# Attention stage: turning before the scores, Y turned back one unit at a time, two buffers for Y^T

## Chip, cores, metric

One core of one Trainium2 chip. The metric is the device time of one execution in microseconds. The program is a chain of stages (four layers) in one launch; the change is in one stage, the attention of layer 0.

## What is computed

Layer 0 is a normalization, three projections, softmax attention with 4 batches of 1024 positions, 16 heads of 32, and an output projection. The stage at hand is this part:

```python
q = (xn @ q_w + q_b).reshape(Bx, Tx, H, -1)
k = (xn @ k_w + k_b).reshape(Bx, Tx, H, -1)
att = jnp.einsum('bnhl,bmhl->bnmh', q, k)
mask = src_mask.reshape(Bx, 1, Tx, 1)
att = att + (1.0 - mask) * -1000000.0
att = jax.nn.softmax(att, axis=2)
v = ((xn @ v_w + v_b) * src_mask[:, :, None]).reshape(Bx, Tx, H, -1)
y = jnp.einsum('bnmh,bmhl->bnhl', att, v).reshape(Bx, Tx, Dx)
```

The other stages (a linear attention, two selective scans, their projections) are not touched.

## The kernel before

The work of the stage is cut into units: one unit is 128 queries of one head of one batch, against all 1024 keys, so U = 4 x 16 x 8 = 512 units. Four units make a group (G = 128), two a pair. q, k and v come in two parts each, a high and a low one, so that products at TensorE's faster fp32r type are exact enough. The queue SP loads q and k (ring of three), v and the mask row.

There is no planner. Each engine's order is written out by hand as a loop over u, and semaphores (`w(engine, name, count)`) hold the engines together.

- **TensorE** (L749 to L816): `scores(u)` makes S in two matmuls of 512 columns, into one of two PSUM buffers, once `shifted` says that the unit two before has been read. `turn(u)` transposes the probabilities `pr` in eight transpositions of 128x128 into the single PSUM buffer TP; it waits for `exped` (the unit's exponential) and, half by half, for `lo_taken` (the half of TP is free). `weigh(u)` does eight matmuls of 256 columns, half of those of a pair, that sum v^T p^T into YT, high and low part in turn. `turn_back(g)` multiplies the copied Y^T of four units by `fold`, which adds the two 32-row halves and turns Y back, into the single PSUM buffer Y; it waits for `yt_copied` and `y_ready`. Its contraction runs over 64 rows, that of all the others over 128.
- **VectorE** (L818 to L862): `shift(u)` adds the mask, takes the maximum and writes `sm`; `take_lo(u)` makes the low part of p^T in two halves from TP and the high part; `take(g)` divides Y of four units by the sums of the exponentials (a reciprocal and a multiplication).
- **ScalarE** (L864 to L891): the exponential of a unit, `copy_hi(u)` (the high part of p^T in two halves, out of TP), and `copy_yt(g)` (YT to SBUF, `yts`).

In the loop of TensorE the scores are three units ahead, and the weighing two behind. In the loop of VectorE the low part is of the unit before, the shift two ahead. ScalarE does the exponential of u, then the high part of u - 1, and in every fourth unit the copy of Y^T.

Of the kernel before, what the change touches and what calls it, by code (L numbers as in the profile page):

```python
# [19 lines left out]
P = 128  # L20
B, T, D = 4, 1024, 512
E = 1024
H, DH = 16, 32
# [636 lines left out]
def attention(core, ident, io, scr):  # L660
# [3 lines left out]
    nc = core.nc  # L664
    with ExitStack() as ctx:
        sb, psum = allocator(nc, ctx, "att")
        ring = lambda n, count, shape: [sb(f"{n}{j}", shape) for j in range(count)]
# [3 lines left out]
        fold = sb("fold", [2 * DH, DH])  # L671
# [1 line left out]
        psums = sb("psums", [P, 16])  # L673
        pT = [ring(f"pT{part}", 2, [P, 2, T]) for part in ("hi", "lo")]
        rden = sb("rden", [P, 4])
        yts = sb("yts", [2 * DH, 4, P])
        y = ring("y", 2, [P, TT, D])
        S = [psum(f"S{j}", [P, T]) for j in range(2)]
        TP = psum("TP", [P, T])
        YT = psum("YT", [2 * DH, 4, P])  # L680
        Y = psum("Y", [P, 4, DH])
# [6 lines left out]
        U = B * H * TT  # L688
# [59 lines left out]
        @block.tensor  # L748
        def _(pe):  # L749
            def scores(u):  # L750
                n, t = u // TT, u % TT
                if t == 0:
                    pe.wait_ge(kq_in[n % 3].handle, kq_in[n % 3].at(128 * (n // 3 + 1)))
                if u >= 2:
                    w(pe, "shifted", u - 1)
                for c in range(2):
                    last = nc.tensor.matmul(S[u % 2][:, c * HALF:(c + 1) * HALF], q[n % 3][:, t * P:(t + 1) * P].bitcast(F32R),
                                            k[n % 3][:, c * HALF:(c + 1) * HALF].bitcast(F32R), start=True, stop=True)
                last.then_inc(s["scored"].handle, 1)

            def turn(u):
                w(pe, "exped", u + 1)
                for half in range(2):
                    if u >= 1:
                        w(pe, "lo_taken", 2 * u - 1 + half)
                    for m in range(4 * half, 4 * half + 4):
                        last = nc.tensor.transpose(TP[:, m * P:(m + 1) * P], pr[u % 2][:, m * P:(m + 1) * P], ident[:])  # L767
                    last.then_inc(s["turned"].handle, 1)

            def weigh(u):  # L770

                def of(pair, keys):
                    for m in keys:
                        for part in range(2):
                            last = nc.tensor.matmul(YT[:, pair * 2 % 4:pair * 2 % 4 + 2, :],  # L775
                                                    v[n // 4 % 2][:, m, n % 4, :].bitcast(F32R),
                                                    pT[part][pair % 2][:, :, m * P:(m + 1) * P].bitcast(F32R),
                                                    start=(m == 0 and part == 0), stop=(m == TT - 1 and part == 1))
                    return last

                pair, g = u // 2, u // 4
                n = pair * 2 // TT
                if u % 2 == 0:
                    w(pe, "lo_taken", 2 * u + 4)
                    if u % (4 * TT) == 0:
                        c = n // 4
                        pe.wait_ge(v_in[c % 2].handle, v_in[c % 2].at(16 * (c // 2 + 1)))
                    if u % 4 == 0 and g >= 1:
                        w(pe, "yt_copied", g)
                    of(pair, range(0, TT // 2))  # L790
                else:
                    of(pair, range(TT // 2, TT)).then_inc(s["weighed"].handle, 2)

            def turn_back(g):
                w(pe, "yt_copied", g + 1)
                if g >= 1:
                    w(pe, "y_ready", g)
                for n in range(4):
                    last = nc.tensor.matmul(Y[:, n, :], yts[:, n, :], fold[:], start=True, stop=True)
                last.then_inc(s["y_turned"].handle, 1)  # L800

            w(pe, "fold_ready", 1)
            scores(0)
            scores(1)
            scores(2)
            for u in range(U):
                if u + 3 < U:
                    scores(u + 3)
                turn(u)
                if u >= 2:  # L810
                    weigh(u - 2)
                if u >= 7 and u % 4 == 3:
                    turn_back((u - 7) // 4)
            weigh(U - 2)
            weigh(U - 1)
            turn_back(G - 1)  # L816

        @block.vector  # L818
        def _(dve):
            def shift(u):  # L820
                b = u // (H * TT)
                if u % (H * TT) == 0:
                    w(dve, "mneg_ready", b + 1)
                w(dve, "scored", u + 1)
                if u >= 2:
                    w(dve, "exped", u - 1)
                nc.vector.tensor_tensor_reduce(sm[u % 2][:], S[u % 2][:], mneg[b % 2][:], -1.0, HUGE,  # L827
                                               ALU.add, ALU.min, nmax[u % 2][:]).then_inc(s["shifted"].handle, 1)

            def take_lo(u):  # L830
                for half in range(2):
                    cols_ = slice(half * HALF, (half + 1) * HALF)
                    w(dve, "hi_copied", 2 * u + half + 1)
                    nc.vector.tensor_tensor(pT[1][u // 2 % 2][:, u % 2, cols_].bitcast(F32R), TP[:, cols_],  # L834
                                            pT[0][u // 2 % 2][:, u % 2, cols_], ALU.subtract).then_inc(s["lo_taken"].handle, 1)

            def take(g):
                b, h, first = g // (2 * H), g // 2 % H, g % 2 * 4
                at = g % 4 * 4
                w(dve, "y_turned", g + 1)  # L840
                nc.vector.reciprocal(rden[:], psums[:, at:at + 4]).then_inc(core.vector_step.handle, 1)
                dve.wait_ge(core.vector_step.handle, core.vector_step.at(g + 1))
                if g % (2 * H) == 0 and b >= 2:
                    dve.wait_ge(y_stored[b % 2].handle, y_stored[b % 2].at(16 * (b // 2)))
                nc.vector.tensor_tensor(y[b % 2][:, first:first + 4, h * DH:(h + 1) * DH], Y[:],
                                        rden[:].unsqueeze(2).broadcast_to([P, 4, DH]), ALU.mult
                                        ).then_inc(s["y_ready"].handle, 1)

            nc.vector.tensor_tensor(fold[:], ident[0:2 * DH, 0:DH], ident[0:2 * DH, DH:2 * DH], ALU.add
                                    ).then_inc(s["fold_ready"].handle, 1)  # L850
            shift(0)
            shift(1)
            for u in range(U):
                if u >= 1:
                    take_lo(u - 1)
                if u + 2 < U:
                    shift(u + 2)
                if u >= 9 and u % 4 == 1:
                    take((u - 9) // 4)
            take_lo(U - 1)  # L860
            take(G - 2)
            take(G - 1)  # L862

        @block.scalar  # L864
        def _(act):
            def copy_hi(u):
                if u >= 4:
                    w(act, "weighed", u // 2 * 2 - 2)
                for half in range(2):
                    cols_ = slice(half * HALF, (half + 1) * HALF)  # L870
                    w(act, "turned", 2 * u + half + 1)
                    nc.scalar.copy(pT[0][u // 2 % 2][:, u % 2, cols_].bitcast(F32R), TP[:, cols_]).then_inc(s["hi_copied"].handle, 1)  # L872

            def copy_yt(g):
                w(act, "weighed", 4 * g + 4)
                if g >= 1:
                    w(act, "y_turned", g)
                nc.scalar.copy(yts[:], YT[:]).then_inc(s["yt_copied"].handle, 1)

            for u in range(U):  # L880
                w(act, "shifted", u + 1)
                if u >= 2:
                    w(act, "turned", 2 * u - 2)
                if u % 4 == 0 and u >= 16:
                    w(act, "y_ready", u // 4 - 3)
                at = u % 16
                nc.scalar.activation(pr[u % 2][:], sm[u % 2][:], ACT.Exp, bias=nmax[u % 2][:, 0:1], scale=-1.0,  # L887
                                     accum_out=psums[:, at:at + 1]).then_inc(s["exped"].handle, 1)
                if u >= 1:
                    copy_hi(u - 1)  # L890
                if u >= 6 and u % 4 == 2:  # L891
                    copy_yt((u - 6) // 4)
            copy_hi(U - 1)
            copy_yt(G - 1)
# [1044 lines left out]
```

## Time and profile before

| | |
|---|---|
| median of 3 runs | 7576.78 us (7569.86 to 7577.42) |
| profiled execution | 7567.35 us |
| its span, first to last instruction | 7565.6 us |
| share of the span busy: PE, PEld, DVE, ACT, POOL | 80%, 54%, 66%, 59%, 33% |
| mean granted clock of TensorE over the span | 0.922 |
| attention stage, first turn to last | 576.6 to 1972.9 us |

PE is TensorE's matmuls, PEld its weight loads, DVE VectorE, ACT ScalarE. The costliest groups of the whole program are those of the scans, which lie in other stages; the rows below are of the attention stage, except where a row of another stage shows the same kind of step. Matmuls are pipelined and the end of one is modelled, so distances between starts are read, not durations. In the timeline neighbouring instructions of one kind are merged (x8), and a short stretch is asked for where single ones matter. "issue" is time in which the engine waited for nothing that the profile shows.

### The profile page before, as it was taken

The numbers are of one execution on the slowest core, as the hardware profiler recorded it, in microseconds if no ns is written. First come the engines' busy times: TensorE is split into PE (matmuls) and PEld (weight loads), VectorE is DVE, ScalarE is ACT, GpSimd is POOL, SyncE is SP. The second block draws the span as 40 slices with busy tenths as digits, with TensorE's granted clock in tenths as the row PEclk, the third lists the DMA queues.
The fourth block names the chain that finished last, engine by engine and source line by source line (L and its number), as shares of the span: only waits on it lengthen the run. The fifth ranks groups of instructions, "written<-read, shape, count | busy, mean of one in ns | idle before, by whom it ended". The sixth has DMA issues, their size and how long they took to land. (4 is left out here: it accounts for less than half of the span.)

```text
span 7565.6 us, 90723 instructions
## 1 busy us (share of the span) xinstructions
PE 6062.6 (80%) x31488; PEld 4117.5 (54%) x31488; DVE 5014.9 (66%) x6337; ACT 4501.4 (59%) x6759; POOL 2519.9 (33%) x1130
## 2 busy tenths in 40 slices
PE   4899999999568945599957888887499957888884
PEld 1338888888433443344436666665244446666662
DVE  2338999999541153344459999996344479999993
ACT  2118888888510042244458888885344469888991
POOL 0000000000000000000039999996100059999994
PEclk8999999999789977799979999999799979999997
DMA  5443232222353244533355555653433355655554
GB/s 192 192 155 77 64 75 73 65 68 62 122 191 138 94 165 182 200 124 147 121 164 139 154 147 160 161 153 92 163 128 132 135 165 145 163 154 149 149 150 164
DMA packets 615822, 1035.65 MB, mean 137 GB/s; under 512 B 105817, under 2 KB 253401, under 8 KB 608741
## 3 DMA queue, kind: packets, MB, share of 16 engines
q1 hardware_dynamic: 600484, 954.60, 41.3%
q10 hardware_dynamic: 9792, 58.85, 1.9%
q0 software_dynamic: 5120, 16.78, 0.6%
q8 instruction: 236, 3.87, 0.2%
q14 instruction: 190, 1.55, 0.1%
HBM read 640.74 MB, written 389.31 MB: 136 GB/s over the span
## 5 line engine op out<-in xcount | busy, mean ns | idle before, releaser
L1570 POOL TENSOR_TENSOR scan_hC<-scan_h,scan_Crep 128x1024 f32<-128x1024 f32 x1024 | 2395.0, 2367 | 3491.6 <-DVE scan_h L1740 3421.8
L1613 PE MATMUL scan_y<-ident,scan_hC 128*128 128x128 f32 x8192 | 1136.5, 283 | 369.6 <-POOL scan_hC L1570 365.1
L1690 ACT ACTIVATE scan_a<-scan_dt,scan_A 128x512 f32<-128x512 f32 x2048 | 1352.2, 694 | 48.9 <-DVE scan_h L1740 45.3
L1740 DVE TENSOR_TENSOR_SCAN scan_h<-scan_a,scan_carry,scan_h 128x512 f32<-128x512 f32 x1024 | 1220.0, 1261 | 57.7 <-ACT scan_a L1690 55.0
L1740 DVE TENSOR_TENSOR_SCAN scan_h<-scan_a,scan_h 128x512 f32<-128x512 f32 x1024 | 1161.1, 1201 | 109.7 <-ACT scan_a L1690 107.0
L1666 ACT COPY scan_h<-scan_drive 128x1024 f32<-128x1024 f32 x1024 | 1040.2, 1016 | 299.0 <-PE scan_drive L1601 279.9
L1613 PEld LDWEIGHTS scan_y<-ident,scan_hC 128*128 128x128 f32 x8192 | 908.3, 143 | 529.2 <-POOL scan_hC L1570 461.7
L1601 PE MATMUL scan_drive<-scan_Bd,scan_dT 128*128 128x256 f32 x4096 | 878.2, 337 | 138.3 <-ACT scan_h L1666 82.3
L1601 PEld LDWEIGHTS scan_drive<-scan_Bd,scan_dT 128*128 128x128 f32 x4096 | 598.8, 195 | 410.9 <-issue 248.6
L834 DVE TENSOR_TENSOR att_pTlo<-att_TP,att_pThi 128x512 fp32r<-128x512 f32 x1024 | 657.9, 684 | 128.3 <-ACT att_pThi L872 126.5
L872 ACT CAST att_pThi<-att_TP 128x512 fp32r<-128x512 f32 x1024 | 547.2, 586 | 179.7 <-PE att_TP L767 173.1
L827 DVE CUSTOM_DVE_ANT_0 att_sm<-att_S,att_mneg 128x1024 f32<-128x1024 f32 x512 | 621.5, 1214 | 13.0 <-POOL att_mneg L745 12.8
L887 ACT ACTIVATE att_pr<-att_sm,att_nmax 128x1024 f32<-128x1024 f32 x512 | 592.9, 1158 | 46.5 <-DVE att_nmax L827 46.5
L521 PE MATMUL p_bank<-p_W,p_xT 128*128 128x512 f32 x1280 | 557.7, 597 | 51.8 <-DMA p_xT<-scratch_xT 48.5
L767 PE MATMUL att_TP<-ident,att_pr 128*128 128x128 f32 x4096 | 566.6, 279 | 24.8 <-DVE att_pTlo L834 24.7
L767 PEld LDWEIGHTS att_TP<-ident,att_pr 128*128 128x128 f32 x4096 | 453.3, 141 | 184.9 <-issue 116.3
L1639 PE MATMUL scan_O<-scan_Wo,scan_gT 128*128 128x512 f32 x1024 | 536.9, 617 | 5.4 <-ACT scan_gT L1697 5.4
L775 PE MATMUL att_YT<-att_pThi,att_v 128*64 128x256 f32 x2048 | 538.6, 298 | 0.0
L1188 PE MATMUL ssmin_ring<-ssmin_xT,ssmin_Wx 128*128 128x512 f32 x1024 | 472.7, 619 | 70.4 <-DMA ssmin_xT<-scratch_xT 53.3
L775 PE MATMUL att_YT<-att_pTlo,att_v 128*64 128x256 f32 x2048 | 496.2, 277 | 0.0
L1188 PE MATMUL ssmin_ring<-ssmin_Wz,ssmin_xT 128*128 128x512 f32 x1024 | 459.2, 599 | 11.6 <-ACTq L1253 11.6
L745 POOL TENSOR_SCALAR att_mneg<-att_mrow 128x1024 f32<-128x1024 f32 x4 | 14.5, 3636 | 1348.8 <-DMA att_mrow<-mask 1348.8
(142 smaller groups left out, 6804.1 us busy)
## 6 DMA issues: line engine op xcount, KB each, us to landing
scan_dT<-scratch_dtuT SPq DMA_DIRECT2D x512, 256.0 KB, 4.9
scratch_dtuT<-ssmin_dT SPq DMA_DIRECT2D x128, 512.0 KB, 2.9
scan_Crep<-scratch_bc SPq DMA_DIRECT2D x64, 1024.0 KB, 10.7
scratch_xT<-n_xT ACTq DMA_DIRECT2D x24, 2048.0 KB, 7.4
p_xT<-scratch_xT SPq DMA_DIRECT2D x16, 2048.0 KB
att_q<-scratch_q_split SPq DMA_DIRECT2D x256, 128.0 KB, 3.0
att_k<-scratch_k_split SPq DMA_DIRECT2D x256, 128.0 KB, 3.2
scratch_uD<-ssmin_uD SPq DMA_DIRECT2D x64, 512.0 KB, 4.4
```

The source lines that it names most:

```text
L767: last = nc.tensor.transpose(TP[:, m * P:(m + 1) * P], pr[u % 2][:, m * P:(m + 1) * P], ident[:])
L775: last = nc.tensor.matmul(YT[:, pair * 2 % 4:pair * 2 % 4 + 2, :], v[n // 4 % 2][:, m, n % 4, :].bitcast(F32R), pT[part][pair % 2][:, :, m ...
L827: nc.vector.tensor_tensor_reduce(sm[u % 2][:], S[u % 2][:], mneg[b % 2][:], -1.0, HUGE, ALU.add, ALU.min, nmax[u % 2][:]).then_inc(s["shif ...
L834: nc.vector.tensor_tensor(pT[1][u // 2 % 2][:, u % 2, cols_].bitcast(F32R), TP[:, cols_], pT[0][u // 2 % 2][:, u % 2, cols_], ALU.subtract ...
L887: nc.scalar.activation(pr[u % 2][:], sm[u % 2][:], ACT.Exp, bias=nmax[u % 2][:, 0:1], scale=-1.0, accum_out=psums[:, at:at + 1]).then_inc( ...
L1188: last = nc.tensor.matmul(ring[o % 4][:], lhs, rhs, start=(kt == 0), stop=(kt == KT - 1))
L1570: nc.gpsimd.tensor_tensor(hC[k % 2][:], of, Crep[:, 2 * p:2 * p + 2, :], ALU.mult).then_inc(s["scaled"].handle, 1)
L1601: last = nc.tensor.matmul(drive[:, c * TC:(c + 1) * TC, :], dT[j][:, at * P:(at + 1) * P].bitcast(F32R), Bd[th][:, at, :, first:first + GS ...
L1613: last = nc.tensor.matmul(y[j][:, t, :], hC[k % 2][:, i, t * P:(t + 1) * P], ident[:], start=(p == 0 and i == 0 and t == 0), stop=False, i ...
L1666: nc.scalar.copy(h[group % 3][:, :, tt * P:(tt + 1) * P], drive[:].rearrange("p t n -> p n t")).then_inc(s["laid"].handle, 1)
L1690: nc.scalar.activation(a[(2 * k + i) % 3][:], dt[j][:], ACT.Exp, scale=A[:, m, 2 * p + i:2 * p + i + 1]).then_inc(s["decayed"].handle, 1)
L1740: nc.vector.tensor_tensor_scan(of, a[(2 * k + i) % 3][:], of, first, ALU.mult, ALU.add).then_inc(s["scanned"].handle, 1)
```

## The change

Three edits in `attention`. TensorE's loop calls `turn(u)` before `scores(u + 3)`, not after. `turn_back` works on one unit instead of four, in every round from u = 7 on, each raising `y_turned`; the waits stand before the first piece of a group. `yts` becomes a ring of two, and `copy_yt(g)` waits for the block of g - 2 instead of g - 1. VectorE's `take` moves from behind the shift in rounds with u % 4 = 1 to ahead of the shift in rounds with u % 4 = 3, and waits for four pieces.

```diff
-        yts = sb("yts", [2 * DH, 4, P])
+        yts = ring("yts", 2, [2 * DH, 4, P])
...
-            def turn_back(g):
-                w(pe, "yt_copied", g + 1)
-                if g >= 1:
-                    w(pe, "y_ready", g)
-                for n in range(4):
-                    last = nc.tensor.matmul(Y[:, n, :], yts[:, n, :], fold[:], start=True, stop=True)
-                last.then_inc(s["y_turned"].handle, 1)
+            def turn_back(u):
+                g = u // 4
+                if u % 4 == 0:
+                    w(pe, "yt_copied", g + 1)
+                    if g >= 1:
+                        w(pe, "y_ready", g)
+                nc.tensor.matmul(Y[:, u % 4, :], yts[g % 2][:, u % 4, :], fold[:], start=True, stop=True
+                                 ).then_inc(s["y_turned"].handle, 1)
...
             for u in range(U):
+                turn(u)
                 if u + 3 < U:
                     scores(u + 3)
-                turn(u)
                 if u >= 2:
                     weigh(u - 2)
-                if u >= 7 and u % 4 == 3:
-                    turn_back((u - 7) // 4)
+                if u >= 7:
+                    turn_back(u - 7)
             weigh(U - 2)
             weigh(U - 1)
-            turn_back(G - 1)
+            for u in range(U - 7, U):
+                turn_back(u)
...
-                w(dve, "y_turned", g + 1)
+                w(dve, "y_turned", 4 * g + 4)
...
                 if u >= 1:
                     take_lo(u - 1)
+                if u >= 11 and u % 4 == 3:
+                    take((u - 11) // 4)
                 if u + 2 < U:
                     shift(u + 2)
-                if u >= 9 and u % 4 == 1:
-                    take((u - 9) // 4)
...
-                if g >= 1:
-                    w(act, "y_turned", g)
-                nc.scalar.copy(yts[:], YT[:]).then_inc(s["yt_copied"].handle, 1)
+                if g >= 2:
+                    w(act, "y_turned", 4 * g - 4)
+                nc.scalar.copy(yts[g % 2][:], YT[:]).then_inc(s["yt_copied"].handle, 1)
```

TensorE before, from the end of a weighing in a round with u % 4 = 3 into the next round (L799 is the turning back, L757 the scores, L767 the turn, L775 the weighing):

```order
L775 MATMUL att_YT<-att_pTlo,att_v 64x256
L799 MATMUL att_Y<-att_fold,att_yts 128x32 [waits y_ready,yt_copied]
L799 MATMUL att_Y<-att_fold,att_yts 128x32 x3
L757 MATMUL att_S<-att_k,att_q 128x512 [waits shifted]
L757 MATMUL att_S<-att_k,att_q 128x512
L767 MATMUL att_TP<-ident,att_pr 128x128 [waits lo_taken,exped]
L767 MATMUL att_TP<-ident,att_pr 128x128 x3
L767 MATMUL att_TP<-ident,att_pr 128x128 [waits lo_taken]
L767 MATMUL att_TP<-ident,att_pr 128x128 x3
L775 MATMUL att_YT<-att_pThi,att_v 64x256 [waits lo_taken]
```

TensorE in the changed kernel, from the end of a weighing in any round into the next (L800 is the turning back):

```order
L775 MATMUL att_YT<-att_pTlo,att_v 64x256
L800 MATMUL att_Y<-att_fold,att_yts 128x32
L767 MATMUL att_TP<-ident,att_pr 128x128 [waits lo_taken,exped]
L767 MATMUL att_TP<-ident,att_pr 128x128 x3
L767 MATMUL att_TP<-ident,att_pr 128x128 [waits lo_taken]
L767 MATMUL att_TP<-ident,att_pr 128x128 x3
L757 MATMUL att_S<-att_k,att_q 128x512 [waits shifted]
L757 MATMUL att_S<-att_k,att_q 128x512
L775 MATMUL att_YT<-att_pThi,att_v 64x256
```

A single matmul on `yts` now stands between each weighing and the next turn, and the scores stand between the turn and the weighing.

VectorE before and in the changed kernel, at the take (L834 and L836 are the low part, L827 and L829 the shift, L841 and L845, L843 and L847 the take):

```order
L834 TENSOR_TENSOR att_pTlo<-att_TP,att_pThi 128x512 [waits hi_copied] x2
L827 ISA att_sm,att_nmax<-att_S,att_mneg 128x1024 [waits exped,scored]
L827 ISA att_nmax 128x1
L841 RECIPROCAL att_rden<-att_psums 128x4 [waits y_turned]
L845 TENSOR_TENSOR att_y<-att_Y,att_rden 128x4x32 [waits vector_step]
L834 TENSOR_TENSOR att_pTlo<-att_TP,att_pThi 128x512 [waits hi_copied] x2
```

```order
L836 TENSOR_TENSOR att_pTlo<-att_TP,att_pThi 128x512 [waits hi_copied] x2
L843 RECIPROCAL att_rden<-att_psums 128x4 [waits y_turned]
L847 TENSOR_TENSOR att_y<-att_Y,att_rden 128x4x32 [waits vector_step]
L829 ISA att_sm,att_nmax<-att_S,att_mneg 128x1024 [waits exped,scored]
L829 ISA att_nmax 128x1
```

The take stands ahead of a shift now, not ahead of a low part.

## Rows read from the trace of the kernel before

**Rows 1.** Windows of the attention stage: busy us (x instructions) by engine, granted clock, DMA
```profile
577.00:1973.00 1396.00, 1371.22 (x10192) 1183.04 (x10191) 1263.89 (x2294) 1184.60 (x2172) 10.90 (x3) 1.00 0.26 65
```
**Rows 2.** Timeline, PE, two blocks of Y; columns: start us, us, engine, line, operation
```profile
1000.91 0.28 PE L775 MATMUL att_YT<-att_pTlo,att_v 128*64 128x256 f32 x1
1001.12 1.08 PE L799 MATMUL att_Y<-att_fold,att_yts 64*128 64x32 f32 x8
...
1002.70 0.27 PE L767 MATMUL att_TP<-ident,att_pr 128*128 128x128 f32 x1
...
1012.05 1.07 PE L799 MATMUL att_Y<-att_fold,att_yts 64*128 64x32 f32 x8
```
**Rows 3.** Timeline, PE and PEld, a unit and the next turn
```profile
1004.38 0.30 PEld L757 LDWEIGHTS att_S<-att_k,att_q 128*128 128x128 f32 x2
1004.49 0.63 PE L757 MATMUL att_S<-att_k,att_q 128*128 128x512 f32 x2
...
1004.96 1.05 PE L767 MATMUL att_TP<-ident,att_pr 128*128 128x128 f32 x8
...
1006.66 0.28 PE L775 MATMUL att_YT<-att_pTlo,att_v 128*64 128x256 f32 x1
...
1006.77 0.64 PE L757 MATMUL att_S<-att_k,att_q 128*128 128x512 f32 x2
...
1007.57 0.96 PEld L767 LDWEIGHTS att_TP<-ident,att_pr 128*128 128x128 f32 x8 [0.60 <-issue]
```
**Rows 4.** Timeline, PE, where the number of rows changes (short stretches)
```profile
1001.25 0.38 PE L799 MATMUL att_Y<-att_fold,att_yts 64*128 64x32 f32 x2
...
1001.92 0.27 PE L799 MATMUL att_Y<-att_fold,att_yts 64*128 64x32 f32 x1
1002.12 0.50 PE L757 MATMUL att_S<-att_k,att_q 128*128 128x512 f32 x1
...
3272.76 0.59 PE L1188 MATMUL ssmin_ring<-ssmin_Wz,ssmin_xT 128*128 128x512 f32 x1
3273.28 0.69 PE L1219 MATMUL ssmin_DTP<-ssmin_xd,ssmin_Wdt 64*128 64x512 f32 x1
...
3273.82 1.45 PE L1219 MATMUL ssmin_DTP<-ssmin_xd,ssmin_Wdt 64*128 64x512 f32 x3
```
**Rows 5.** Timeline, ACT and DVE, the same group
```profile
1005.65 1.07 ACT L872 CAST att_pThi<-att_TP 128x512 fp32r<-128x512 f32 x2
...
1006.35 0.17 DVE L841 RECIPROCAL att_rden<-att_psums 128x4 f32<-128x4 f32 x1
...
1006.77 1.28 DVE L834 TENSOR_TENSOR att_pTlo<-att_TP,att_pThi 128x512 fp32r<-128x512 f32 x2
...
1006.98 0.58 ACT L878 COPY att_yts<-att_YT 64x512 f32<-64x512 f32 x1 [0.25 <-PE att_YT L775]
1007.46 1.15 ACT L887 ACTIVATE att_pr<-att_sm,att_nmax 128x1024 f32<-128x1024 f32 x1
...
1007.97 1.21 DVE L827 CUSTOM_DVE_ANT_0 att_sm<-att_S,att_mneg 128x1024 f32<-128x1024 f32 x1
...
1008.60 1.05 ACT L872 CAST att_pThi<-att_TP 128x512 fp32r<-128x512 f32 x2
...
1009.11 0.08 DVE L827 DVE_READ_ACCUMULATOR2_ANT att_nmax<- 128x1 f32 x1
...
1009.20 1.29 DVE L834 TENSOR_TENSOR att_pTlo<-att_TP,att_pThi 128x512 fp32r<-128x512 f32 x2
```
**Rows 6.** Timeline, PEld, the weight loads of the block
```profile
1001.12 0.96 PEld L799 LDWEIGHTS att_Y<-att_fold,att_yts 64*128 64x128 f32 x8 [0.18 <-issue]
```
**Rows 7.** Timeline, PE, the turn of u3: whole, from its fifth matmul, from its sixth
```profile
1010.04 1.16 PE L767 MATMUL att_TP<-ident,att_pr 128*128 128x128 f32 x8
...
1010.54 0.44 PE L767 MATMUL att_TP<-ident,att_pr 128*128 128x128 f32 x2
...
1010.71 0.38 PE L767 MATMUL att_TP<-ident,att_pr 128*128 128x128 f32 x2
```

## The prediction

> **What bounds the kernel now.** I read the stage's windows first, then the instructions in order of time for one group of four units, and last the rows in which TensorE changes its kind of work. The edit touches nothing outside the attention stage. There TensorE shows a matmul in flight for 98% of the time at a granted clock of 1.00 [rows 1]; since matmuls overlap, that share does not say that it never waits. The stage is very regular: the block that turns Y back starts at 1001.12 and again at 1012.05 [rows 2], so a group takes 10.93 us, and 128 groups make 1399 us of the 7565.6 us span.
>
> Where do the 10.93 us go? Name the units of a group u0 to u3. A unit in which nothing waits takes 2.26 us, from the turn of u0 at 1002.70 to that of u1 at 1004.96 [rows 2, 3]. The block costs what lies between the last weighing matmul at 1000.91 and the next turn at 1002.70 [rows 2], 1.79, less the ordinary step after that matmul (0.11, 1006.66 to 1006.77) and less two scores (0.47, 1004.49 to 1004.96) [rows 3]: 1.21 us. Four units and the block are 9.04 + 1.21 = 10.25 us. The other 0.68 us are waits, 87 us over the stage. The largest is seen at the turn of u2: its weight load stands 0.60 us [rows 3]. It is labelled "issue", but it starts (1007.57) 0.80 us after VectorE began the low part of the unit before (1006.77) [rows 5], and the turn needs the half of the buffer TP that this frees. So this is a loop: turn, high part on ScalarE, low part on VectorE, next turn. It is late there because VectorE had first to do the take (reciprocal at 1006.35, low part at 1006.77) [rows 5].
>
> **What a piece costs.** The block holds 8 hardware matmuls (each of the four comes as two) on weights of 64 rows, in the midst of work on 128 rows. Every change of the row count shows. Into the block: 0.21 us from the last weighing to the first Y instead of 0.11, and 0.13 to the second Y (1001.12 to 1001.25) instead of the 0.11 between later ones [rows 2, 4]: 0.11 us in all. Out of it: 0.20 us from the last Y (1001.92) to the first score (1002.12), and 0.58 for the two scores up to 1002.70 instead of 0.47 [rows 2, 4]: 0.09 + 0.10. That this goes with the row count and not with one wait is seen in the stage that makes the inputs of the scans: 128 rows to 64, with 512 columns, takes 0.52 (3272.76 to 3273.28) and then 0.54 us, where the later steps take 0.43 (three matmuls in 1.45, less the 0.59 that one lasts, by two) [rows 4], so again 0.09 and some 0.10. In these rows the new weight load starts with its matmul (load at 1001.12, matmul at 1001.12), while at equal rows it runs ahead (load at 1004.38, matmul at 1004.49) [rows 2, 3, 6].
>
> The change makes eight changes of the row count per group out of two. Four of them are weighing to Y, 0.11 each, measured. The other four are Y to a turn, which the trace does not have. A lower bound is nothing, if transpositions could load ahead. An upper bound is what the scores pay, 0.19. A price from the nearest rows: the start is 0.09 late as in every other case, and the first transposition then pays its own uncovered load, which is seen where the fifth one of a turn waits: 0.17 us to the next (1010.54 to 1010.71) instead of 0.11, so 0.055. I take 0.145 [rows 4, 7]. A piece is then 0.11 + 2 x 0.11 + 0.145 = 0.48 us, four are 1.91 against 1.21 for the block: 0.70 us more TensorE work per group, 90 us over the stage. That it all counts follows from the floor: 9.04 + 1.91 = 10.95 us per group, already what the group takes now with its waits. The change can pay only by removing the 0.68 us, and that only gets it to even.
>
> **Which waits stay.** With pieces a unit lasts 2.26 + 0.48 = 2.74 us. The turn's loop needs 0.69 (turn at 1004.96 to high part at 1005.65 [rows 3, 5]), 0.60 (high part at 1008.60 to low at 1009.20) and 0.84 (low part at 1009.20 to turn at 1010.04) [rows 5, 7], together 2.1: no wait in an undisturbed unit, and a take of 0.42 (1006.35 to 1006.77) fits as well. But one disturbance grows. ScalarE's copy of Y^T stands ahead of the next exponential and waits for a weighing that now ends later after its turn, since the scores stand between. Walk from the turn of u1 as zero: turn 0.87 + 0.055, scores 0.47, eighth weighing matmul at 1.40 + 7 x 0.115 = 2.20; copy 0.32 later (1006.66 to 1006.98) at 2.52; exponential 0.48 later (1007.46) at 3.00; high part of u2 1.14 later (1008.60) at 4.14; low part at 4.74; turn of u3 at 5.58 [rows 3, 5, 7]. Two units without a wait would put it at 5.48: 0.10 us of wait. VectorE goes on from there: two low parts (1.20) to 5.94, the take 0.42, the shift 1.14 (1007.97 to 1009.11, where its maximum is read out), low part of u3 at 7.50, turn of the next u0 at 8.34 against 5.58 + 2.74 = 8.32: 0.02 more [rows 5]. Next u1 at 11.08. Second halves of the turns, which wait for the second low part with a margin of some hundredths, may add up to 0.06. I take 11.12 us per group.
>
> The rest is free. The second Y^T buffer removes a wait of the copy on the block, which has long ended by then. The take waits for the fourth piece, whose second matmul starts at 2.74 + 2.20 + 0.34 = 5.28 and which lets go about 0.4 later, ahead of 5.94; if it were later, the shift behind it would slip as much. Y has one buffer: the first piece of a group waits for that take, which ends over a microsecond earlier. The scores behind the turn feed a shift three units on. The other three pieces at the end of the stage and the first turn ahead of the fourth scores are under 1 us. SP's and POOL's streams do not move.
>
> **The sum.** 11.12 - 10.93 = 0.19 us, x 128 = +24 us. On the profiled execution's own 7567.35 us that is 7591; on the median of the three runs, 7576.8 (0.12% above it), it is **7601 us**, 0.3% slower. About 0.2%, 15 us, is what a measurement of this kernel can tell from no change.
>
> **The rivals.** *B, not slower: the change back to transpositions is free.* Then a unit is 2.59 us. The walk has no 0.055, the turn of u3 falls at 5.52, that of the next u0 at 8.28, of the next u1 at 10.87: 0.06 less than now, -8 us, 7569. For it speaks that no row shows this transition; against it, that all others cost 0.09 at the start, whichever kinds of matmul stand on its sides. It decides from a transition under about 0.10 us: at 0.09 the same walk gives 10.97 and +5 us.
>
> The trace has load and matmul starting together wherever the rows change. The Trainium skill (TensorE: Matmul & The Clock Gate, "Step-by-step: what each phase is for") says that TensorE pulls a weight load ahead of running matmuls when the row groups don't conflict or the load goes to the background buffer. By it all eight changes could be free, and the walk would still be held by the same chain over ScalarE's copy, the take and the shift at 10.87 or a little over it, so 7569 to 7572. Rows 4 and 6 speak against it, and the measured rows decide.
>
> *C, a turn pays as the scores do or more.* At 0.19 a unit is 2.785 us and the group 11.19: +33 us, 7610. If the fall into a turn also costs what its two waits cost when the queue is not ahead (0.06 more), no chain matters any more and the group is 4 x 2.845 = 11.38: +58 us, 7634. For it: the turn is led by two semaphore waits. Against: TensorE's stream reads them ahead, as after the block today, where nothing is lost.
>
> *D, faster: the pieces cost only their share of the block and turning first removes every wait.* 4 x 2.26 + 1.21 = 10.25 us, -87 us, 7490. It would need two changes of rows instead of eight; the order shows eight.
>
> **How the numbers follow.** My forecast of 7586 to 7618 (group 11.0 to 11.25) gets 0.64, B 0.17, C above 7618 0.15, D 0.04. The range takes in the forecast, B from 7572 on, and C but for its top: 7572 to 7628. Faster by over 0.2% is D with a sliver of B, 0.05; within 0.2%, to 7592, is B and the lower end of the forecast, 0.22; slower 0.73.
>
> **What would show it.** In the changed trace: groups 11.1 us apart; 0.21 us from weighing to every Y; 0.20 from the second Y matmul to a turn that did not wait, and 0.16 within it; ScalarE idle some 0.8 us ahead of the copy instead of 0.25; waits of the turns down from 0.68 to 0.1 or 0.2 per group; DVE's low part of u2 over 1 us idle. A group under 10.95, or Y to turn at 0.11, proves the main term wrong; a wait of the first piece on y_ready or of an exponential on the take would prove the free part wrong.

## The result, and the profile after

The changed kernel takes 7595.49 us (median of 7 runs, 7589.5 to 7600.39), the kernel before in the same comparison 7569.86 us (7563.45 to 7577.42). The ratio is 1.0034 with a 95% interval of 1.0024 to 1.0044; forecast were 24 us more and a ratio of 1.0032. The profiled execution took 7600.39 us, its span 7598.6 us.

A stretch of 1200 us inside the attention stage (columns: the stretch, then busy us and instructions of PE, PEld, DVE, ACT and POOL, granted clock, share of DMA, GB/s), kernel after:

```profile
600.00:1800.00 1200.00, 1197.89 (x8611) 1021.48 (x8609) 1067.02 (x1939) 1009.47 (x1829) 7.27 (x2) 1.00 0.27 66
```

A group is 80 matmuls (8 of scores, 32 of turns, 32 of weighing, 8 of Y), so 1200 us by 8611 / 80 are 11.15 us per group, where 10.93 stood before [rows 2]. The difference, 0.22 us, times 128 is 28 us; the runs show 26. TensorE's busy share has risen from 98% [rows 1] to 99.8%, at the same clock of 1.00: it waits less and takes longer.

The timeline of TensorE for a group (columns: start us, us, engine, line, operation), kernel after:

```profile
1002.96 1.09 PE L767 MATMUL att_TP<-ident,att_pr 128*128 128x128 f32 x8
1003.81 0.71 PE L757 MATMUL att_S<-att_k,att_q 128*128 128x512 f32 x2
1004.36 0.28 PE L775 MATMUL att_YT<-att_pThi,att_v 128*64 128x256 f32 x1
...
1005.71 1.09 PE L767 MATMUL att_TP<-ident,att_pr 128*128 128x128 f32 x8
...
1008.46 1.09 PE L767 MATMUL att_TP<-ident,att_pr 128*128 128x128 f32 x8
...
1011.29 1.16 PE L767 MATMUL att_TP<-ident,att_pr 128*128 128x128 f32 x8
1012.21 0.71 PE L757 MATMUL att_S<-att_k,att_q 128*128 128x512 f32 x2
```

Turns of u0, u1 and u2 at 1002.96, 1005.71 and 1008.46 are 2.75 us apart, with no wait. The turn of u3 comes 2.83 us after that of u2. The walk had 2.74 us per unit, and 0.10 us of wait ahead of u3. From the turn of u0 to the scores are 0.85 us and from there to the weighing 0.55, where the walk had 0.925 and 0.47: the sum of 1.40 is right, its division is not.

The same place in short stretches, so that single matmuls stand apart, and the weight loads there:

```profile
1002.42 0.28 PE L775 MATMUL att_YT<-att_pTlo,att_v 128*64 128x256 f32 x1
1002.63 0.29 PE L800 MATMUL att_Y<-att_fold,att_yts 64*128 64x32 f32 x1
...
1002.76 0.27 PE L800 MATMUL att_Y<-att_fold,att_yts 64*128 64x32 f32 x1
...
1003.13 0.38 PE L767 MATMUL att_TP<-ident,att_pr 128*128 128x128 f32 x2
```

```profile
1002.63 0.29 PEld L800 LDWEIGHTS att_Y<-att_fold,att_yts 64*128 64x128 f32 x2 [0.18 <-issue]
...
1002.96 0.86 PEld L767 LDWEIGHTS att_TP<-ident,att_pr 128*128 128x128 f32 x8
```

From the last weighing to the first Y 0.21 us, and 0.13 to the second; from that 0.20 to the first transposition, and 0.17 from it to the second. Against the steps of 0.11 us, the transition that no row of before showed costs 0.09 at the start and about 0.06 in the first transposition, where 0.145 in all was assumed. The loads start with their matmuls there, as at the block before [rows 6].

The chain to the turn of u3, ScalarE and VectorE in the same group:

```profile
1008.23 0.58 ACT L880 COPY att_yts<-att_YT 64x512 f32<-64x512 f32 x1 [0.69 <-PE att_YT L775]
...
1008.71 1.15 ACT L889 ACTIVATE att_pr<-att_sm,att_nmax 128x1024 f32<-128x1024 f32 x1
...
1009.86 1.05 ACT L874 CAST att_pThi<-att_TP 128x512 fp32r<-128x512 f32 x2
...
1010.45 1.29 DVE L836 TENSOR_TENSOR att_pTlo<-att_TP,att_pThi 128x512 fp32r<-128x512 f32 x2 [0.95 <-ACT att_pThi L874]
```

With the turn of u1 at 1005.71 as zero, copy, exponential, high part and low part lie at 2.52, 3.00, 4.15 and 4.74, and the turn of u3 at 5.58 (1011.29): each within a hundredth of the walk of the prediction. The reciprocal of the take follows at 5.95 (1011.66), 5.94 in the walk. Where the time of ScalarE and of the turns' loads went, by the waits summed over 1200 us (columns: engine, tile and line, what it waited for, us in total, times, longest):

```profile
ACT att_yts L880 <- PE att_YT L775: 74.8, 108, 0.7
...
PEld att_TP L767 <- issue: 0.2, 1, 0.2
```

ScalarE waits 0.69 us for each of 108 weighings, where it waited 0.25 before [rows 5] and some 0.8 was forecast; VectorE stands 0.95 us ahead of the low part of u2, forecast was over 1. The turns' loads, one of which stood 0.60 us [rows 3], now wait for 0.2 us in 1200; the tenth of a microsecond at u3 is too short to be listed.

### The profile page after: what moved, and what is told of

Same layout as the page of the kernel before. It is cut to its first block and busy times, and to the rows that moved or that the text cites. A ratio compares the mean times of both kernels' runs of the same rounds, so it can differ in the third digit from the quotient of the medians.

```text
span 7598.6 us, 90722 instructions
## 1 busy us (share of the span) xinstructions
PE 6103.3 (80%) x31488; PEld 4141.6 (55%) x31488; DVE 5014.8 (66%) x6337; ACT 4514.7 (59%) x6759; POOL 2520.0 (33%) x1130
## 5 line engine op out<-in xcount | busy, mean ns | idle before, releaser
L836 DVE TENSOR_TENSOR att_pTlo<-att_TP,att_pThi 128x512 fp32r<-128x512 f32 x1024 | 658.4, 685 | 154.8 <-ACT att_pThi L874 154.6
L829 DVE CUSTOM_DVE_ANT_0 att_sm<-att_S,att_mneg 128x1024 f32<-128x1024 f32 x512 | 621.8, 1215 | 14.0 <-POOL att_mneg L745 13.3
L767 PE MATMUL att_TP<-ident,att_pr 128*128 128x128 f32 x4096 | 570.9, 281 | 4.4 <-DVE att_pTlo L836 2.0
L775 PE MATMUL att_YT<-att_pThi,att_v 128*64 128x256 f32 x2048 | 496.0, 278 | 0.3 <-DVE att_pTlo L836 0.3
L775 PE MATMUL att_YT<-att_pTlo,att_v 128*64 128x256 f32 x2048 | 494.3, 277 | 0.0
L767 PEld LDWEIGHTS att_TP<-ident,att_pr 128*128 128x128 f32 x4096 | 437.2, 141 | 49.4 <-issue 3.4
```

## Experiments

Each was timed beside the kernel before on the same chip; ratios are to that. Group times are from the same window: 1200 us divided by an 80th of its PE matmuls.

**Pieces over 128 rows (e1).** Y^T and `fold` get 64 more rows, which are zero, so that the product is the same and TensorE's row count never changes.

```diff
-        fold = sb("fold", [2 * DH, DH])
+        fold = sb("fold", [P, DH])
-        yts = ring("yts", 2, [2 * DH, 4, P])
+        yts = ring("yts", 2, [P, 4, P])
...
-            nc.vector.tensor_tensor(fold[:], ident[0:2 * DH, 0:DH], ident[0:2 * DH, DH:2 * DH], ALU.add
+            nc.vector.tensor_tensor(fold[:], ident[:, 0:DH], ident[:, DH:2 * DH], ALU.add
                                     ).then_inc(s["fold_ready"].handle, 1)
+            for j in range(2):
+                nc.vector.tensor_copy(yts[j][2 * DH:P].rearrange("p n t -> p (n t)"), ident[2 * DH:P, 0:1].broadcast_to([P - 2 * DH, 4 * P])
+                                      ).then_inc(s["fold_ready"].handle, 1)
...
-                nc.scalar.copy(yts[g % 2][:], YT[:]).then_inc(s["yt_copied"].handle, 1)
+                nc.scalar.copy(yts[g % 2][0:2 * DH], YT[:]).then_inc(s["yt_copied"].handle, 1)
```

> The changed kernel, but the contraction of the pieces runs over 128 rows (fold and Y^T padded with zero rows), so TensorE never changes its row count. Theory R (each change of the row count costs 0.09 us and an uncovered load): a piece falls from 0.48 to 0.22 us, the unit to 2.49 us; the chain over ScalarE's copy, the take and the shift then holds the group at 10.9 us (now 11.15): 30 us less than the changed kernel, within 0.1% of the kernel before. Theory W (a piece is dear because it is a short matmul of its own, or because of the semaphore waits around it, whatever its rows): group stays at 11.15, time equal to the changed kernel's.

Measured: 7541.51 us, ratio 0.9982 (0.9972 to 0.9991). Timeline of TensorE and the window:

```profile
1004.83 1.07 PE L767 MATMUL att_TP<-ident,att_pr 128*128 128x128 f32 x8
...
1007.13 0.30 PE L800 MATMUL att_Y<-att_fold,att_yts 128*128 128x32 f32 x2
1007.27 1.07 PE L767 MATMUL att_TP<-ident,att_pr 128*128 128x128 f32 x8
...
1010.39 1.16 PE L767 MATMUL att_TP<-ident,att_pr 128*128 128x128 f32 x8 [0.51 <-DVE att_pTlo L836]
...
600.00:1800.00 1200.00, 1137.38 (x8856) 1030.95 (x8855) 1091.47 (x1993) 1038.26 (x1881) 7.28 (x2) 1.00 0.27 67
```

The group takes 10.84 us (8856 matmuls); expected were 10.9 and a time within 0.1% of the kernel before, and it is 0.2% faster. Two Y matmuls and the step to the turn are 0.14 us (1007.13 to 1007.27) where they were 0.33 (1002.63 to 1002.96 after). Theory R holds and W falls: the same pieces, in the same places and with the same semaphore waits in the code, are cheap once the row count stays. A unit without a wait takes 2.44 us (turns at 1004.83 and 1007.27), 0.31 less than in the changed kernel and 0.05 less than R had it. A wait of 0.51 us appears at the turn of u3: from the turn of u1 it still takes 5.56 us (1004.83 to 1010.39), the chain, which the dear pieces had nearly covered.

**The block of four again (e2).** `turn_back` as before the change; turn first, take and the two buffers stay.

```diff
-                if u >= 7:
-                    turn_back(u - 7)
+                if u >= 7 and u % 4 == 3:
+                    turn_back((u - 7) // 4)
```

> The changed kernel with Y turned back in one block of four again, behind the weighing of rounds with u % 4 = 3; turn first, take and two Y^T buffers stay. If only the row changes had cost (R alone, no new wait): four units 9.04 and the block 1.21, group 10.3 us, 80 us faster than the kernel before. With the chain from the turn of u1 over weighing, copy of Y^T, exponential, high part and low part to the turn of u3 (5.53 us whatever the pieces cost, against 4.52 for two bare units) the group is 11.3 us: slower than the changed kernel by some 20 us and than the kernel before by some 45 us.

Measured: 7606.06 us, ratio 1.0070 (1.0053 to 1.0087).

```profile
999.95 1.04 PE L767 MATMUL att_TP<-ident,att_pr 128*128 128x128 f32 x8
...
1002.23 1.10 PE L767 MATMUL att_TP<-ident,att_pr 128*128 128x128 f32 x8
...
1005.49 1.16 PE L767 MATMUL att_TP<-ident,att_pr 128*128 128x128 f32 x8 [0.78 <-DVE att_pTlo L834]
...
600.00:1800.00 1200.00, 1119.11 (x8457) 988.36 (x8456) 1046.91 (x1901) 991.66 (x1797) 7.27 (x2) 1.00 0.26 65
```

Group 11.35 us (8457). With two row changes instead of eight the kernel is slower still, 51 us more than before where some 45 were expected. From the turn of u2 (1002.23) to that of u3 (1005.49) are 3.26 us where a bare unit takes 2.26; TensorE waits 0.78 us there for the low part. So the row changes alone are not the story: the chain from the turn of u1 (999.95) to that of u3 takes 5.54 us, as it does with the pieces (5.58) and was expected (5.53), and what two pieces cost there is time that would be waited anyway.

**Scores ahead of the turn again (e3).** The two lines of the loop in the old order; pieces, take and buffers of the changed kernel.

> The changed kernel with the scores ahead of the turn again, as before the change; pieces, take and buffers stay. R: every piece now stands between a weighing and a score, 0.11 + 0.22 + 0.19 = 0.52 us, the unit is 2.79 us without any wait, the group 11.15 us: same time as the changed kernel. If the turn ahead of the scores is what costs (through the later weighing and the copy), the group falls towards 10.9 us or below, 30 us or more less.

Measured: 7592.15 us, ratio 1.0049 (1.0032 to 1.0066).

```profile
1003.31 0.41 PE L800 MATMUL att_Y<-att_fold,att_yts 64*128 64x32 f32 x2
1003.65 0.73 PE L757 MATMUL att_S<-att_k,att_q 128*128 128x512 f32 x2
1004.22 1.03 PE L767 MATMUL att_TP<-ident,att_pr 128*128 128x128 f32 x8
...
1007.02 1.04 PE L767 MATMUL att_TP<-ident,att_pr 128*128 128x128 f32 x8
...
600.00:1800.00 1200.00, 1200.00 (x8572) 1042.95 (x8571) 1072.04 (x1931) 997.98 (x1822) 7.26 (x2) 1.00 0.26 66
```

Group 11.20 us (8572). The turns are 2.80 us apart (1004.22, 1007.02), four of which are the group, and TensorE shows a matmul in flight all the time. Each piece now leads into a score, 0.34 us from the first Y to the score and 0.57 for the two scores instead of 0.47 [rows 3]. With these pieces turning first is thus worth 0.05 us per group: its way out of a piece is 0.05 us cheaper four times, less what it loses at u3. It is no gain on a wait, since e3 has none, and the two whole times do not tell the kernels apart (ratios 1.0034 and 1.0049, their intervals overlap).

**The kernel before with a block over 128 rows (e4).** The padding of e1 on the single `yts`, nothing else.

> The kernel before, with the block of Y over 128 rows (fold and Y^T padded with zero rows), nothing else. R: the block falls from 1.21 to 0.90 us and the group from 10.93 to 10.63: 39 us less than the kernel before. W: no change.

Measured: 7515.69 us, ratio 0.9947 (0.9930 to 0.9963).

```profile
1003.17 0.97 PE L799 MATMUL att_Y<-att_fold,att_yts 128*128 128x32 f32 x8
1003.98 0.71 PE L757 MATMUL att_S<-att_k,att_q 128*128 128x512 f32 x2
1004.53 1.04 PE L767 MATMUL att_TP<-ident,att_pr 128*128 128x128 f32 x8
...
600.00:1800.00 1200.00, 1178.41 (x9038) 1038.10 (x9037) 1119.56 (x2034) 1048.86 (x1922) 7.27 (x2) 1.00 0.28 70
```

Group 10.62 us (9038). The block takes 0.81 us to the next score (1003.17 to 1003.98) instead of 1.00 (1001.12 to 1002.12 [rows 2, 4]), and the two scores 0.55 instead of 0.58. The two row changes of a group are worth 40 us of the kernel before; expected were 39.

**Copy of Y^T behind the exponential (e5).** On the changed kernel.

```diff
                 if u >= 1:
                     copy_hi(u - 1)
-                if u >= 6 and u % 4 == 2:
-                    copy_yt((u - 6) // 4)
```

```diff
+                if u >= 7 and u % 4 == 3:
+                    copy_yt((u - 7) // 4)
                 if u >= 1:
                     copy_hi(u - 1)
```

> The changed kernel with ScalarE's copy of Y^T one place later: behind the exponential of rounds with u % 4 = 3, no longer ahead of it. If the remaining waits of the changed kernel come from the copy that holds up that exponential, they vanish, every unit is at its floor of 2.745 us (2.26 + 0.11 + 0.22 + 0.15) and the group takes 10.98 instead of 11.15 us: 22 us less than the changed kernel, still 5 us more than the kernel before, since row changes alone fill the group. If the waits have another cause (take ahead of the shift), the group stays at 11.15.

Measured: 7575.61 us, ratio 1.0011 (1.0001 to 1.0020).

```profile
1002.64 1.09 PE L767 MATMUL att_TP<-ident,att_pr 128*128 128x128 f32 x8
...
1010.88 1.09 PE L767 MATMUL att_TP<-ident,att_pr 128*128 128x128 f32 x8
...
600.00:1800.00 1200.00, 1200.00 (x8740) 1039.25 (x8739) 1101.94 (x1967) 1023.43 (x1858) 7.27 (x2) 1.00 0.27 67
```

Three units take 8.24 us (1002.64 to 1010.88), 2.75 each, with no wait of the turns in the trace; group 10.98 us (8740), as expected. The remaining waits were the copy's; without them the changed kernel is at the floor of its pieces, and that floor is above the 10.93 of before. The whole time is 9 us above the kernel before, and by the ratios 17 us under the changed kernel, where 5 and 22 were expected.

**Turn first alone (e9).** The kernel before, with only the order of turn and scores changed.

> The kernel before with nothing changed but the order of turn and scores. If turning first shortens the loop over the single buffer TP (the reason that one would give for the edit), the 0.68 us of waits shrink and the group falls below 10.93 us. By the chain over the copy of Y^T it grows: the weighing now ends 0.47 us later after its turn, so does the copy, and with it the exponential, the high part and the turn of u3: group 11.3 us, 45 to 50 us more than the kernel before.

Measured: 7608.46 us, ratio 1.0070 (1.0053 to 1.0087).

```profile
1001.25 1.04 PE L767 MATMUL att_TP<-ident,att_pr 128*128 128x128 f32 x8
...
1003.87 1.16 PE L767 MATMUL att_TP<-ident,att_pr 128*128 128x128 f32 x8 [0.19 <-DVE att_pTlo L834]
...
1006.78 1.16 PE L767 MATMUL att_TP<-ident,att_pr 128*128 128x128 f32 x8 [0.38 <-DVE att_pTlo L834]
...
600.00:1800.00 1200.00, 1142.01 (x8465) 984.46 (x8464) 1048.08 (x1904) 980.94 (x1798) 7.27 (x2) 1.00 0.26 65
```

Group 11.34 us (8465); 51 us more than before, expected were 45 to 50. The turn at 1001.25 is that of u1. The steps into u2 (2.62 us) and into u3 (2.91 us) hold waits for the low part; before, they were 2.64 and 2.44 [rows 3, 5, 7]. Turning first does not shorten the loop over TP; it makes the weighing, and with it the copy, later, and from the turn of u1 to that of u3 it now takes 5.53 us instead of 5.08 (1004.96 to 1010.04 [rows 3, 7]).

**Combinations (e6, e7, e8).** e6 is e1 with the scores first. e8 is e6 with the copy moved as in e5. e7 is e1 with the copy moved, the pieces eight units back, and the take behind the shift of rounds with u % 4 = 0:

```diff
-                if u >= 7:
-                    turn_back(u - 7)
+                if u >= 8:
+                    turn_back(u - 8)
...
-                if u >= 11 and u % 4 == 3:
-                    take((u - 11) // 4)
                 if u + 2 < U:
                     shift(u + 2)
+                if u >= 12 and u % 4 == 0:
+                    take((u - 12) // 4)
```

> Pieces over 128 rows as in e1, and the scores ahead of the turn again. The chain from the turn of u1 to the turn of u3 then holds no scores between turn and weighing: 5.1 instead of 5.5 us. Group 10.4 to 10.5 us, 60 us less than the kernel before and 45 us less than e1. If the order of turn and scores didn't matter, it would be e1's time (group 10.85).

Measured: 7504.01 us, ratio 0.9915 (0.9898 to 0.9932), group 10.43 us (9208): 63 us less than before, expected were 60.

```profile
1005.35 1.03 PE L767 MATMUL att_TP<-ident,att_pr 128*128 128x128 f32 x8
...
1010.41 0.41 PE L767 MATMUL att_TP<-ident,att_pr 128*128 128x128 f32 x2
...
600.00:1800.00 1200.00, 1199.90 (x9208) 1061.09 (x9206) 1139.82 (x2071) 1080.13 (x1956) 7.27 (x2) 1.00 0.28 70
```

These are the turns of u1 and u3: without the scores between turn and weighing the chain takes 5.06 us, where e1 has 5.56. With cheap pieces the order that the change gave up is worth 0.41 us per group (10.84 to 10.43).

> As e1 (pieces over 128 rows, seven units back, the changed kernel's take), with the scores ahead of the turn and the copy of Y^T moved as in e5. One wait of 0.12 us per group is left, at a turn behind the take: group 10.05 to 10.1 us, 105 to 112 us less than the kernel before, a little more than e7.

Measured: 7465.63 us, ratio 0.9869 (0.9853 to 0.9885), group 10.14 us (9463): the expected 105 to 112 us came out as 101.

```profile
1001.18 0.57 ACT L883 COPY att_yts<-att_YT 64x512 f32<-64x512 f32 x1
...
1001.86 0.13 PEld L775 LDWEIGHTS att_YT<-att_pThi,att_v 128*64 128x64 f32 x1 [0.19 <-issue]
...
PEld att_YT L775 <- issue: 23.2, 117, 0.4
...
600.00:1800.00 1200.00, 1199.61 (x9463) 1109.89 (x9463) 1172.87 (x2130) 1089.61 (x2011) 7.27 (x2) 1.00 0.28 72
```

The wait that the sum had, 0.12 us at a turn, is not there; another one is: 117 weight loads of the weighing, one per group, stand 0.2 us each. With the scores ahead of the turn the weighing follows right on the turn, too early for the copy that frees YT and is now one place later (in the rows it starts at 1001.18 and takes 0.57 us; the load starts at 1001.86).

> All three: pieces over 128 rows, turn ahead of the scores, copy of Y^T behind the exponential of rounds with u % 4 = 3, pieces eight units back instead of seven and the take behind the shift of rounds with u % 4 = 0. No wait on TensorE: four units of 2.26 + 0.22, group 9.93 to 10.0 us, 120 to 128 us less than the kernel before. If TensorE isn't the only bound (VectorE needs 9.8 us per group by its rows), the group ends between 10.0 and 10.4.

Measured: 7439.61 us, ratio 0.9831 (0.9815 to 0.9848), 127 us less than the kernel before, and the fastest of all.

```profile
1003.24 0.28 PE L775 MATMUL att_YT<-att_pTlo,att_v 128*64 128x256 f32 x1
1003.24 0.31 PEld L800 LDWEIGHTS att_Y<-att_fold,att_yts 128*128 128x128 f32 x2
1003.36 0.30 PE L800 MATMUL att_Y<-att_fold,att_yts 128*128 128x32 f32 x2
1003.39 0.27 PE L800 MATMUL att_Y<-att_fold,att_yts 128*128 128x32 f32 x1
1003.50 1.07 PE L767 MATMUL att_TP<-ident,att_pr 128*128 128x128 f32 x8
1004.32 0.48 PE L757 MATMUL att_S<-att_k,att_q 128*128 128x512 f32 x1
...
600.00:1800.00 1200.00, 1199.87 (x9684) 1115.90 (x9683) 1194.54 (x2179) 1113.48 (x2058) 7.27 (x2) 1.00 0.29 72
```

Group 9.91 us (9684). Four units of 2.44, as e1 has one without a wait, would be 9.76. VectorE is busy for 1194.54 of the 1200 us, so that it has no room left either; whether it is what makes the group 0.15 us longer than that was not tried. e7 turns first, so that the scores stand between turn and weighing, and the trace lists no wait of the weighing as in e8. How the step from e8 to e7 divides between the order, the pieces' place and that of the take was not tried.

## Why the prediction was right

- **The main term.** 0.70 us more TensorE work per group for the pieces. The rows after show a piece as forecast (0.21, 0.13, 0.20, 0.17), e5 shows the floor without waits at 10.98 us against 10.95, and e1 and e4 show that the price goes with the row count: 0.31 us per group in either (11.15 to 10.84, 10.93 to 10.62). In e1 eight changes went and gave back no more than two in e4, since the chain took over; its undisturbed unit alone is 0.31 us shorter, which would be 1.24 per group. How the price divides was misread: the prediction put 0.11 to the way into 64 rows and 0.145 to the way back to a turn, and against the same steps over 128 rows they are 0.19 and 0.12 (last section). It did no harm to the forecast, which added up whole steps as they were measured.
- **The transition without a row**, Y to a turn at 0.145, was right: 0.09 and 0.06 were measured. The row that gave the 0.055 was the fifth transposition after a wait [rows 7]. Rival B, which needed it under 0.10, falls with it. At a change of rows the loads start with their matmuls and not ahead of them (1002.63 and 1002.96). The Trainium skill (TensorE: Matmul & The Clock Gate, "Step-by-step: what each phase is for") names conditions for pulling a load ahead; the prediction's reading that by them all eight changes could be free is the one that falls. e1 has no change of rows at all, and is 14 us under the kernel before, where the prediction gave that case 5 to 8.
- **The chain over the copy.** Each of its five points lies where the walk had it. e2, e9 and e5 show it from three sides: 11.35 and 11.34 us with blocks and turn first, 10.98 with the copy out of its way. It takes 5.53 to 5.58 us wherever the turn is first and the copy ahead of the exponential (after, e1, e2, e9), and 5.06 in e6 with the scores first.
- **What was short.** 11.12 us were taken and 11.15 measured. Part of it is in the steps rounded to a hundredth (units of 2.75 instead of 2.74), part in the turn of u3, whose second half waits: it takes 0.92 us to the scores instead of 0.85 (1011.29 to 1012.21), where the forecast had taken 0.04 of an allowance of up to 0.06.
- **Rival C** needed 0.19 for the way into a turn, as the scores pay; the changed kernel shows 0.15 there, and e3, which has the scores in that place, takes 11.20 us. **Rival D** needed cheap pieces and no wait from turning first; e2, with the block's price and turn first, takes 11.35 us instead of its 10.25.

## What to carry to other kernels

Before a short matmul is scattered among others, compare the rows of its contraction with theirs: the price is paid at each change, so a block pays it twice and four pieces eight times. Padding with zero rows removed it here, and no run shows a price for that (e1, e4). And when work is put between two steps of a loop, follow every engine that waits for the later one: in the kernel before, the low part of u2 starts as the shift ahead of it ends (1009.20, after the read-out of 0.08 at 1009.11) and 0.60 us after its high part (1008.60) [rows 5], about the 0.59 us of the changed kernel, where VectorE waits for ScalarE (1009.86 to 1010.45). So the chain over the copy and VectorE's own work came out even, and nothing was in reserve: of the 0.47 us of scores put ahead of the weighing, 0.45 arrived at the turn of u3 (e9). Moving the copy by one place gave back 0.17 us per group (e5).

## What the runs showed of the hardware

A change between 64 and 128 contraction rows makes TensorE load the next weights late. In the changed kernel the load for the first Y matmul starts with that matmul, 0.21 us after the last weighing matmul (1002.42, 1002.63); in e7, at equal rows, it starts together with the last weighing matmul and 0.12 us ahead of its own (1003.24, 1003.36). What follows, changed kernel against e7:

- into 64 rows: 0.21 instead of 0.12 us to the first Y matmul, 0.13 instead of 0.03 to the second, so 0.19 in all;
- back to 128 rows: 0.20 instead of 0.11 us to the turn, and 0.85 instead of 0.82 from the turn to the scores, so 0.12.

The sum is the 0.31 us by which the undisturbed units differ (2.75 and 2.44 in e1). In e4 the ways in and out come once per group, for 0.31 us too.

The prediction took the 0.13 us to the second Y matmul as nearly its ordinary step, since later Y matmuls are 0.11 us apart. They are so over 128 rows as well (e4: six steps from 1003.20 to 1003.86); only the second comes quickly there. The loads of the two are 0.11 or 0.12 us apart in either kernel (changed: 1002.63 and 1002.74; e7: 1003.24 and 1003.36), but in e7 the first stands 0.12 us ahead of its matmul. That is why two Y matmuls and the step to the turn take 0.14 us in e7 (1003.36 to 1003.50), where 0.22 were reckoned, and why e7 could come out at 9.91 us instead of 9.93 or more. How much of e1's 10.84 instead of 10.9 comes from it isn't shown, since the chain holds e1.

Every kind of change that was met had the late start (weighing to Y, Y to scores, Y to turn, and 128 to 64 rows at 512 columns [rows 4]); what happens in it was not tried.
